# A fused attention and feed-forward layer on eight cores: two edits, odd transposed tiles of the probabilities copied by ScalarE, and the next group's transposes issued after the fourth output tile

## What is computed

```python
h = layernorm(x)
y = einsum('bsh,oh->bso', h, W_qkv).reshape(*h.shape, 3)
q, k, v = y[..., 0], y[..., 1], y[..., 2]
attn = softmax(einsum('bqh,bkh->bqk', q, k) / sqrt(1024))
x = x + layernorm(einsum('bsh,oh->bso', einsum('bqk,bkh->bqh', attn, v), W_out))
h = layernorm(x)
e = gelu(h @ w1 + b1) @ w2 + b2            # 1024 -> 4096 -> 1024
e = e * sum(renormalised top-2 router weights of h)
x = x + layernorm(e)
```

## Time and profile before

| | us |
|---|---|
| median of 2 runs | 1789.78 |
| lowest, highest | 1789.72, 1789.84 |
| the profiled execution, whole | 1775.19 |
| its span on the slowest core (core 2) | 1773.6 |
| span of the eight cores | 1763.5 to 1773.6 |
| TensorE busy | 1440.8 (81%) |
| ScalarE busy | 629.5 (35%) |
| VectorE busy | 468.1 (26%) |

### The profile page before, as it was taken

One profiled execution on the slowest core, in us unless ns is written; L12 is line 12 of the kernel. 1 busy time (PEld: TensorE's weight loads), 2 busy tenths in 40 slices (PEclk: granted clock), 3 DMA queues, 4 the chain that ended last, 5 costly groups with the idle time before them and its releaser, 6 DMA issues.

```text
span 1773.6 us, 19543 instructions; the slowest of 8 cores (1763.5 to 1773.6 us)
## 1 busy us (share of the span) xinstructions
PE 1440.8 (81%) x6816; PEld 649.4 (37%) x6816; DVE 468.1 (26%) x1006; ACT 629.5 (35%) x1293; POOL 170.8 (10%) x149
## 2 busy tenths in 40 slices
PE   0588988887788888888888888828986987996896
PEld 0233343333344334444444444313442443443342
DVE  0233333333433333333333333232012011201100
ACT  0532233330223333333333333243534453353334
POOL 1000000000000000000000001120021022012003
PEclk9999999999899888888888888869998998998998
DMA  9311212100401101111111014969022013001002
GB/s 144 65 36 42 48 36 36 25 1 3 87 7 30 30 27 33 26 33 30 32 29 30 30 31 61 171 127 166 1 72 48 1 48 72 0 25 62 10 1 83
DMA packets 51616, 81.54 MB, mean 46 GB/s; under 512 B 19648, under 2 KB 27840, under 8 KB 51520
## 3 DMA queue, kind: packets, MB, share of 16 engines
q0 software_dynamic: 27280, 50.35, 16.4%
q1 hardware_dynamic: 24240, 29.94, 5.4%
HBM read 97.08 MB, written 20.97 MB: 67 GB/s over the span
## 4 chain that ended last, share of the span: by engine, by line
PE 72%; DVE 10%; issue 7%; DMA 5%; ACT 4%; POOL 1%; DVEq 0%; ACTq 0%; POOLq 0%; SPq 0%
PE pAll L185 36%; PE pAll L160 33%; DVE ptb L775 2%; DMA xgb<-xo 2%; PE pAll L216 2%; DMA qs<-qstage 2%; DVE xfg L454 2%; DVE m L702 1%; DVE vt L512 1%; POOL eot L1223 1%; DMA x2lt<-x2s 1%; DVE qstage L482 1%; PE pAll L1087 1%; ACT L1188 1%; PE pAll L1094 0%
## 5 line engine op out<-in xcount | busy, mean ns | idle before, releaser
L160 PE MATMUL pAll<-x2f,w1b 128*128 128x512 bf16 x1024 | 242.4, 401 | 41.3 <-ACT h1g L1188 36.2
L160 PE MATMUL pAll<-kf,qtile 128*128 128x512 bf16 x1024 | 262.3, 418 | 9.4 <-ACT diagb L755 5.4
L185 PE MATMUL pAll<-vt,ptb 128*128 128x512 bf16 x1024 | 225.1, 381 | 0.9 <-DVE ptb L775 0.9
L185 PE MATMUL pAll<-w2b,h1g 128*128 128x512 bf16 x1024 | 222.2, 379 | 4.1 <-ACT h1g L1188 4.1
L702 DVE TENSOR_REDUCE m<-pAll 128x1 f32<-128x512 f32 x128 | 88.6, 692 | 331.1 <-PE pAll L160 329.3
L160 PEld LDWEIGHTS pAll<-x2f,w1b 128*128 128x128 bf16 x1024 | 103.6, 102 | 178.0 <-issue 71.7
L160 PEld LDWEIGHTS pAll<-kf,qtile 128*128 128x128 bf16 x1024 | 108.5, 107 | 152.7 <-issue 55.1
L713 ACT ACTIVATE pbuf<-pAll,nb 128x512 bf16<-128x512 f32 x128 | 87.3, 683 | 174.8 <-DVE nb L707 174.8
L185 PEld LDWEIGHTS pAll<-w2b,h1g 128*128 128x128 bf16 x1024 | 100.0, 98 | 125.7 <-issue 6.3
L185 PEld LDWEIGHTS pAll<-vt,ptb 128*128 128x128 bf16 x1024 | 100.4, 98 | 123.0 <-issue 3.1
L185 PE MATMUL pAll<-wvb,xfg 128*128 128x512 bf16 x512 | 115.7, 379 | 25.4 <-DVE vt L512 25.4
(11 more groups left out here) (111 smaller groups left out, 1174.5 us busy)
## 6 DMA issues: line engine op xcount, KB each, us to landing
xrt<-xo POOLq DMA_DIRECT2D x16, 512.0 KB, 6.0
x2s<-x2t SPq DMA_DIRECT2D x16, 512.0 KB, 3.2
w1b<-w POOLq DMA_DIRECT2D x8, 1024.0 KB, 32.2
w2b<-w POOLq DMA_DIRECT2D x4, 2048.0 KB, 43.8
x2rt<-x2s SPq DMA_DIRECT2D x16, 512.0 KB, 4.5
y<-yt SPq DMA_DIRECT2D x16, 512.0 KB, 2.9
xgb<-xo POOLq DMA_DIRECT2D x16, 256.0 KB, 5.6
qs<-qstage POOLq DMA_DIRECT2D x16, 256.0 KB, 2.6
```

Of the source, the lines that this page charges most:

```text
L160: return e.matmul(o(), l(), r(), start=st, stop=sp)
L185: return e.matmul(o(), l(), r(), start=st, stop=sp)
```

## The change

There are two edits. First, in `emit_tail_transp`, the copies of the four odd batches go from VectorE to ScalarE. Second, `c_pass1(gc+1)` is emitted after the loop over the output tiles, behind k = 3 and all its epilogue, and no longer inside it behind k = 2.

```diff
@@ emit_tail_transp
             dst = ptb[:, b * 512:(b + 1) * 512]
-            ev = read_bank("vector", [bank],
-                           lambda e, d=dst, s=bank.ap: e.tensor_copy(d, s),
-                           waits=fence_pt, inc="vS")
+            if b % 2 == 0:
+                ev = read_bank("vector", [bank],
+                               lambda e, d=dst, s=bank.ap: e.tensor_copy(d, s),
+                               waits=fence_pt, inc="vS")
+            else:
+                ev = read_bank("scalar", [bank],
+                               lambda e, d=dst, s=bank.ap: e.copy(d, s),
+                               waits=fence_pt, inc="sS")
             fence_pt = []
@@ stage C, loop over k
-            if k == 2 and gc + 1 < 4:
-                c_pass1(gc + 1)
+        if gc + 1 < 4:
+            c_pass1(gc + 1)
```

## The result

The changed kernel takes 1816.0 us (median of 11 runs) against 1785.85 (median of 10 runs in the same session; the runs on record before the prediction had 1789.78). The ratio is 1.0163, with a 95% interval of 1.0124 to 1.0202. It is slower, by less than 2% in the middle of its interval, whose upper end just passes 2%. Both medians still count some executions that ran under a lower clock on one die and lasted up to 2028 us; the ratio leaves them out, and without them the medians are 1809.1 and 1779.6.

The account below looks back on a forecast made before the run. TensorE was taken as the bound, 72% of the span, with VectorE's copies bounding stage B's transposes. Stage B 49.6 us slower less 22.8 gained gives 26.8 slower: 1802.0 profiled, 1817 for the median, range 1801 to 1835.

Parts of the forecast that it names:

- The place in ScalarE's list: Stage B transposes: ScalarE's copies wait for the layer norm, so batch 3 waits and scores start 4.4 us later per cycle.
- The rounds behind it: Stage B, after batch 3 starts: two batches take 1.47 us through one bank; scores start 0.49 us behind batch 7.
- The clock in stage B: Stage B scores and projection: low clock costs 3.7 us a cycle; the change was taken to give back 1.0 us.
- its first rival: Stage B: clock gives nothing back, full 4.4 us lost per cycle, 39.8 us slower in all, 1830 us; chance 0.20.
- The last tile: End of stage B: context matmuls start at 1144.2 instead of 1138.88, 5.4 us lost.
- What bounds the transposes: Stage B transposes: VectorE's copies, 0.65 us each, bound the stretch; TensorE waits 2.48 us, then 0.35 us per batch pair.
- The second edit: Stage C group boundaries: moving `c_pass1` removes the 6.08 us gelu wait, keeps 6.01 us of idle; 22.8 us gained.
- The allowance for a low clock in the first blocks: Stage C, block 0 after `c_pass1`: 0.3 us taken off the gain at each boundary.
- That the edit to `c_pass1` gains nothing: Stage C: low clock persists through first blocks and a gelu wait returns; 49.6 us slower, 1839 us; chance 0.06.
- That the copies on ScalarE are not held up: Stage B: batch 3 starts about as now, cycles win some 0.5 us, both edits give 30 us, 1760; chance 0.04.
- The function table's load in block 0: Stage C: ScalarE's 1.28 us load before the first gelu moves behind block 0 and fits under blocks 1 and 2.

Follow-up runs that it names:

- The kernels with one copy: Kernel before, with only batch 1's copy moved to ScalarE: 1.0269 of the time before; with only batch 7's copy moved instead: 1.0012.
- with the layer norm behind: Kernel before with odd copies on ScalarE and the layer norm of two tiles earlier emitted behind the transposes and copies: 0.9806 of the time before.
- the kernel with all copies on VectorE: Kernel before, copies left on VectorE, only the layer norm of two tiles earlier emitted behind the transposes: 0.9851 of the time before.
- the filled changed kernel: Changed kernel plus unused matmuls in the transposes of tiles 2 to 14, 11 ahead of batch 2 and 20 ahead of batch 3: 0.9908 of before.
- the fastest: Kernel before plus odd copies on ScalarE, layer norm behind transposes, `c_pass1` after k = 3's matmuls ahead of its epilogue, and filler matmuls: 0.9439, 1681.1 us.

## Why the prediction was right

It said 1817 us with a range of 1801 to 1835, slower within 2%; measured were 1816.0 and 1.0163. That forecast and median are only 1 us apart is chance. The ratio is the surer comparison: 1817 to 1789.78 is 1.0152. By its steps:

- **The place in ScalarE's list.** Right. Batch 3 starts 7.8 us behind the first batch (663.69 - 655.90), 7.92 were worked out. The wait is 4.31 us and its releaser is the ScalarE copy. The kernels with one copy and with the layer norm behind show that the place is the cause, not the copy.
- **The rounds behind it.** Slightly too dear. The scores start 11.0 to 11.3 us behind the first batch, 11.35 were worked out: batch 3 is 0.13 us earlier than that, two rounds with the ScalarE copy are 1.41 us each instead of 1.47, and the scores follow batch 7 after 0.38 us instead of 0.49. The lost time is 4.1 us a cycle in the mean of the 13 instead of 4.4.
- **The clock in stage B.** The sign was right, the size and its place were not. I took 1.0 us a cycle off, and gave as reason that the projection might keep its clock. It did not: the rows read 5.30 in all cycles but one. What came back was 0.6 us in the scores (5.1 us in the mean of 13 instead of 5.7; 5.21 and 4.99 in the cycles from 655.90 and 703.85). The two errors nearly cancel, and that is luck: 4.1 - 0.6 = 3.5 us a cycle, where the prediction had 4.4 - 1.0 = 3.4. Had the clock given back nothing, the loss would have been 4.1 us a cycle, the very border that the prediction set for its first rival; that the result lies within 2% hung on these 0.6 us.
- **The last tile.** 1188.36 - 1176.58 = 11.8 us from the first batch to the context matmuls, before 1138.88 - 1132.16 = 6.7: 5.1 us lost, predicted 5.4.
- **What bounds the transposes.** The prediction took VectorE's copies for the bound of the whole stretch. That is half right: 1.1 of the first wait of 2.48 us were the layer norm's sum ahead of the first copy, as the kernel with all copies on VectorE shows. The forecast did not suffer, since that sum keeps its place in the changed kernel.
- **The second edit.** Right in the sum and in its parts: the gelu's wait went, the idle time behind the copies' queue stayed, 26.3 us in the mean from the end of k = 3 to the router (39.9 + 0.3 - 13.9 = 26.3). The allowance for a low clock in the first blocks was needed at one boundary: its 56 matmuls take 13.89 us instead of 12.25.
- **The rivals.** That the edit to `c_pass1` gains nothing is refuted by that edit alone, 0.9872. That the copies on ScalarE are not held up holds only when the layer norm is moved; then the gain is even larger, 35 us of stage B, than the 7 us that I had worked out, because the sum on VectorE moves away as well and part of the clock comes back (in the 13 cycles the scores take 5.0 us in the mean instead of 5.7, and the projection keeps its clock in 4 of 15 cycles instead of one).

The function table's load in block 0 stayed without effect: no gelu wait stands behind `c_pass1` in the seven blocks.

## What to carry to other kernels

An instruction moved to an idle engine starts when that engine's list comes to it: read what stands ahead of it in the same cycle, up to the last instruction, before counting its own length, and ask who needs its result next. If another engine has something that nobody waits for (here the layer norm of a tile two cycles back), emit it behind the work on the path; that order was worth 24.5 us of stage B, and the sharing of the work at most 10 more. And count an idle time of TensorE for itself and for what the matmuls behind it may lose in clock (here 1.7 to 2.1 us behind 2.0 to 2.5 us of idle time).

## What the runs showed of the hardware that I had not expected

Idle times of TensorE of 2.0 and 2.5 us cost the kernel before 3.7 us in a cycle of 44.3 us in clock alone, nearly as much as the idle times themselves. With 11 useless matmuls of 512 columns in 2.48 us of idle time the kernel before became 2.2% faster (0.9776), with 9 in 2.0 us elsewhere 1.7% (0.9833). In the 13 cycles from tile 2 on, the same idle time of 2.00 us (2.35 to 2.37 in one cycle each of two of them) lowered the clock of the projection in all 13 before, in all 13 changed, in 8 with the transposes filled, and in one in the filled changed kernel. Whether it does so is not a property of the idle time alone. And filling the long idle times did not always keep the clock: behind transposes with no wait above 0.46 us the scores were low in 2 of 13 cycles of the one kernel (0.9776) and in 3 of 15 of the fastest.
